# A fused transformer, attention and expert kernel: attention stacks transposed by DMA, key tiles taken in pairs, routing spread over two heads

## The reference, cut to what matters

```python
h = tok(x)                    # 8x8 patch convolution: 4 images x 256 tokens of 128; 2 layers; head to 192
h = concatenate([h, txt])     # 4 x 384 = 1536 rows of 192
h = h + attn(layernorm(h))
h = h + ffn(layernorm(h))

# attn; q and v are h @ W + b, reshaped to (NH = 12, BN = 1536, HD = 16)
q = q / maximum(norm(q), 1e-12)
AB = einsum('hnd,hmd->hnm', q, q)
AA = sum(q * q, axis=-1, keepdims=True)
sim = -(AA - 2.0 * AB + swapaxes(AA, -1, -2)) * HD ** (-0.5)
out = einsum('hnm,hmd->hnd', softmax(sim), v)

# ffn: t is the rmsnorm of its input; 16 experts, each row goes to its best 4
top_vals, top_idx = top_k(t @ gate_w.T + gate_b, 4)
route_w = softmax(top_vals)
out = sum over the 4 of route_w * (mlp2(swiglu(mlp1(t))))
```

## Time and profile before

| | us |
|---|---|
| median of 3 runs | 745.86 (744.64 to 749.47) |
| the profiled execution | 744.08 |
| its span in the profile | 742.3 |
| image part, until the first scores | 0 to 235 |
| twelve heads, until the last weighted product ends | 242.5 to 467.6 |
| end of routing and the plan of the tiles | 467.6 to 499.5 |
| experts | 499.5 to 742.3 |

### The profile page before, as it was taken

One profiled execution on the slowest core, in us unless ns is written; L12 is line 12 of the kernel. 1 busy time (PEld: TensorE's weight loads), 2 busy tenths in 40 slices (PEclk: granted clock), 3 DMA queues, 4 the chain that ended last, 5 costly groups with the idle time before them and its releaser, 6 DMA issues.

```text
span 742.3 us, 17563 instructions
## 1 busy us (share of the span) xinstructions
PE 646.7 (87%) x5070; PEld 430.3 (58%) x5071; DVE 450.2 (61%) x1478; ACT 380.0 (51%) x721; POOL 350.4 (47%) x401
## 2 busy tenths in 40 slices
PE   5888899888883999999999999549999999999970
PEld 5776786678651222222222222338999999999960
DVE  0345857675665267777777763446776676767660
ACT  0323337433312799999999999203443444444330
POOL 3111323132332045555555544422778777777781
PEclk9999999999997899999999999759999999999995
DMA  8999999300021992000000000048988998888844
GB/s 331 405 347 300 338 334 319 136 1 1 12 64 53 381 318 101 30 30 30 30 30 30 31 31 33 30 163 265 255 238 232 248 252 231 233 257 235 227 63 76
DMA packets 46064, 124.74 MB, mean 168 GB/s; under 512 B 5243, under 2 KB 31292, under 8 KB 44748
## 3 DMA queue, kind: packets, MB, share of 16 engines
q1 hardware_dynamic: 32780, 108.92, 44.5%
q0 software_dynamic: 11696, 14.19, 9.8%
q10 hardware_dynamic: 1552, 1.18, 0.5%
HBM read 105.53 MB, written 58.42 MB: 221 GB/s over the span
## 4 chain that ended last, share of the span: by engine, by line
PE 59%; DVE 11%; DMA 11%; POOL 7%; issue 5%; ACT 4%; SPq 1%; DVEq 0%; ACTq 0%; POOLq 0%
PE ps L843 14%; PE ps L830 10%; PE ps L982 7%; DMA out<-mid 5%; PE ps L1011 5%; PE ps L992 4%; PE ps L684 3%; DMA odd_sum<-mid 3%; ACT mid L1104 2%; POOL rstd L467 2%; POOL mid L590 2%; DVE stat L1192 2%; DVE mid L1200 2%; PE ps L760 1%; PE ps L657 1%
## 5 line engine op out<-in xcount | busy, mean ns | idle before, releaser
L1104 ACT ACTIVATE mid<-ps 128x1536 f32<-128x1536 f32 x144 | 200.2, 1458 | 29.4 <-PE ps L830 29.4
L843 PE MATMUL ps<-mid 128*32 128x384 f32 x1152 | 123.9, 502 | 1.3
L982 PE MATMUL ps<-mid,big 128*128 128x128 f32 x756 | 99.2, 282 | 0.3 <-ACT mid L1130 0.3
L1534 DVE TENSOR_SCALAR mid<-ps,big 128x128 f32<-128x128 f32 x189 | 54.6, 345 | 69.2 <-PE ps L992 51.9
L982 PEld LDWEIGHTS ps<-mid,big 128*128 128x128 f32 x756 | 91.9, 194 | 4.3 <-ACT mid L1130 0.5
L590 POOL TENSOR_TENSOR mid<-mid 128x384 f32<-128x384 f32 x63 | 68.5, 1087 | 54.1 <-DVE mid L1543 33.5
L830 PE MATMUL ps<-mid 52*128 52x512 f16 x432 | 87.4, 386 | 5.5 <-ACT mid L1104 4.9
L1137 ACT ACTIVATE mid<-mid 128x384 f32<-128x384 f32 x63 | 32.9, 522 | 85.4 <-DVE mid L1534 84.1
L1011 PE MATMUL ps<-big,mid 128*128 x378 | 69.2, 330 | 3.2 <-POOL mid L590 2.9
L541 POOL DMA_INDIRECT expert_in<-big,slot_u x48 | 47.9, 998 | 46.5 <-DVE slot_u L1425 35.5
L1011 PEld LDWEIGHTS ps<-big,mid 128*128 128x128 f32 x378 | 60.4, 190 | 6.3 <-issue 6.2
(11 more groups left out here) (224 smaller groups left out, 1089.8 us busy)
## 6 DMA issues: line engine op xcount, KB each, us to landing
big<-w_cat SPq DMA_DIRECT2D x63, 576.0 KB, 4.0
expert_in<-expert_in SPq DMA_DIRECT2D x16, 1774.5 KB, 48.7
big<-expert_in SPq DMA_DIRECT2D x63, 136.5 KB, 3.6
big<-patches SPq DMA_DIRECT2D x3, 2048.0 KB, 20.5
w_cat<-w_a SPq DMA_DIRECT2D x1, 6144.0 KB, 32.8
big<-w SPq DMA_DIRECT2D x1, 4608.0 KB, 14.6
w_cat<-w_b SPq DMA_DIRECT2D x2, 1536.0 KB, 31.0
big<-patches SPq DMA_DIRECT2D x4, 512.0 KB, 7.4
```

Of the source, the lines that this page charges most:

```text
L843: last = nc.tensor.matmul(oacc[32 * g:32 * g + 32, 0:QW], vhead[par][:, kb, :], probs[kb % 3][:, g * QW:(g + 1) * QW], start=(kb == 0), st ...
L982: last = nc.tensor.matmul(banks[half][:, c * P:(c + 1) * P], w1_t[q][:, half * FF + c * P:half * FF + (c + 1) * P], xtT[r][:, 0:P], start= ...
L1104: nc.scalar.activation(probs[kb % 3], SETS[kb % 2], ACT.Exp, scale=0.5).then_inc(probs_ready, 1)
L1534: last = nc.vector.tensor_scalar(glu[r][:, c * P:(c + 1) * P], bank(1 + r)[:, c * P:(c + 1) * P], b1_cols[:, bass.ds(ex * 6 + c, 1)], 7.0, ...
```

## The change: what it does

1. **Second convolution in front.** `schedule()` swaps two entries, so that the convolution of image 1 comes before the transposes of image 0. Its patches are loaded in four pieces, ahead of the other small loads, and its two row tiles are computed together, piece by piece.
2. **Stacks transposed by DMA.** The PE transposes, the DVE copies and the half precision identity are gone. DVE writes each key column block twice (`key_both`) and two extra query blocks (`qry_more`), and SP issues two DMA transposes per head: 12 blocks of 128x128 for the keys, 8 for the queries. They wait for the stack (`stack_ready`) and until the scores of the head that used the same buffer are done. PE waits for them (`stack_in`) before the first scores of the next head, and DVE before it overwrites the source.
3. **Key tiles in pairs.** Per pair PE does scores kb+2, one step of routing, scores kb+3, weighted kb, weighted kb+1. There are four `probs` buffers.
4. **Routing over two heads.** In head n the output, norms and row of tile n-1 are made, and tile n-2 is transposed, chosen, ranked and scattered. The row and the slots have two buffers. DVE and POOL are reordered to suit; at the end the scatter of tile 10 goes behind the norm powers of tile 11.
5. **Weights in pieces.** `w2` comes in two halves, the copy of `w1_a` in four, that of `w1_b` in two, one piece behind each head's transposes on SP.

```diff
-    return [(*lane[slot - start], b, tiles) for slot in range(len(LANE) + NB - 1)
-            for start, lane, b, tiles in lanes if 0 <= slot - start < len(lane)]
+    order = [(*lane[slot - start], b, tiles) for slot in range(len(LANE) + NB - 1)
+             for start, lane, b, tiles in lanes if 0 <= slot - start < len(lane)]
+    order[1:3] = [order[2], order[1]]
+    return order
...
+        probs4 = carve(QS)
...
-        stk = mid[:, 5 * QS + 2 * KEYB * 32:5 * QS + 2 * KEYB * 32 + NH * STKW].bitcast(f16)
-        key_tok = stk[:, 0:NH * STKW].rearrange("p (h c) -> p h c", h=NH)
-        qry_tok = stk[:, NH * STKW:2 * NH * STKW].rearrange("p (h c) -> p h c", h=NH)
-        stack_pair = [t.rearrange("p (j i) c -> p j (i c)", i=2) for t in (key_tok, qry_tok)]
+        key_flat, qry_flat = stk[:, 0:NH * P], stk[:, NH * P:(NH + 8) * P]
+        key_both = key_flat.rearrange("p (h i c) -> p h i c", h=NH, i=2)
+        key_tok = key_both[:, :, 0, :]
+        qry_tok = qry_flat[:, 0:6 * P].rearrange("p (h c) -> p h c", h=NH)
+        qry_more = qry_flat[:, 6 * P:8 * P].rearrange("p (j c) -> p j c", j=2)
+        qry_late = qry_flat[:, 0:2 * P].rearrange("p (j c) -> p j c", j=2)[:, :, STKW:STKW + STK]
...
+            sp.dma_start(rows_sb, rows[:, 0:5 * D].broadcast_to([P, 5 * D])).then_inc(rows_in, 16)
+            for k in range(0, KT, KT // 4):
+                ks = slice(k, k + KT // 4)
+                sp.dma_start(patch_sb[1][:, ks, :], patches[1][:, ks, :]).then_inc(patch1_in[k * 4 // KT], 16)
+            for dst, src, s in ((cols_sb[:], cols, cols_in), (qkvw_sb, qkv_w, qkvw_in),
...
+            def stacks(n, par):
+
+                sp.wait_ge(stack_ready, n + 1)
+                if n >= 2:
+                    sp.wait_ge(scores_ready, (n - 1) * KEYB)
+                sp.dma_start_transpose(out=keysT[par].rearrange("c (h n) -> c h n", n=P), in_=key_flat).then_inc(stack_in, 16)
+                sp.dma_start_transpose(out=qrysT[par][:, 0:8 * P].rearrange("c (j n) -> c j n", n=P),
+                                       in_=qry_flat).then_inc(stack_in, 16)
...
+                if stage == "S2":
+                    sp.wait_ge(acc_taken, weights_read)
+                    stacks(0, 0)
...
-            sp.wait_ge(vhead_ready, 1)
-            sp.dma_start(w2_sb, w2).then_inc(w_in, 16)
-            sp.dma_start(cat[:, :, 0:768], w1_a.rearrange("p (e c) -> p e c", e=E)).then_inc(w1_joined, 16)
-            for half in range(2):
-                sp.dma_start(cat[HROW * half:HROW * half + CB, :, 768:W1C],
-                             w1_b[0:CB, :].rearrange("p (e c) -> p e c", e=E)[:, :, half * FF:(half + 1) * FF]
-                             ).then_inc(w1_joined, 16)
-
-            sp.wait_ge(tr_taken, tr_base(NT - 2))
             sp.dma_start(b2_sb, b2).then_inc(b2_in, 16)
-
-            sp.wait_ge(w1_joined, 16 * 3)
+            cat, wide = [t.rearrange(f"{a} c -> p e c", **k) for t, a, k in
+                         ((w1_cat, "(e p)", dict(p=P)), (w1_a.rearrange("p (e c) -> e p c", e=E), "e p", {}))]
+            narrow = w1_b[0:CB, :].rearrange("p (e c) -> p e c", e=E)
+            pieces = [(w2_sb[:, k * (E // 2) * 3 * C:(k + 1) * (E // 2) * 3 * C],
+                       w2[:, k * (E // 2) * 3 * C:(k + 1) * (E // 2) * 3 * C], w_in) for k in range(2)]
+            pieces += [(cat[:, e:e + 4, 0:768], wide[:, e:e + 4, :], w1_joined) for e in range(0, E, 4)]
+            pieces += [(cat[HROW * half:HROW * half + CB, :, 768:W1C], narrow[:, :, half * FF:(half + 1) * FF], w1_joined)
+                       for half in range(2)]
+            sp.wait_ge(acc_taken, TOK_ACC)
+            for n in range(1, NT):
+                stacks(n, n % 2)
+                if 2 <= n < 2 + len(pieces):
+                    dst, src, s = pieces[n - 2]
+                    sp.dma_start(dst, src).then_inc(s, 16)
...
+            def pool_head(n, par, old=True, prep2=True):
+
+                pool.wait_ge(oacc_ready, n)
+                head_v(n + 1, 1 - par)
+                if old:
+                    weights(n - 2)
+                if prep2:
                     norm_root(n + 2)
-                if not first:
-                    scatter(r, 1 - par)
+                route(n - 1)
+                route2(n - 1)
+                base_add(n - 1)
+                if old:
+                    scatter(n - 2, par)
...
+            def pe_head(n, par, old=True, last=False):
+                base = head_base(n)
+                first = isinstance(n, int) and n == 0
+
+                def ahead(kb):
+                    if kb < KEYB:
+                        scores(par, kb, n * KEYB + (kb - 1))
                     elif not last:
-                        if kb + 2 == KEYB:
-                            pe.wait_ge(tr_taken, base + (2 if first else 3))
-                        scores(1 - par, kb + 2 - KEYB, n * KEYB + (kb + 1))
+                        scores(1 - par, kb - KEYB, n * KEYB + (kb - 1))
+
+                for kb in range(0, KEYB, 2):
+                    if kb + 2 == KEYB and not last:
+                        pe.wait_ge(stack_in, n * 32 + 64)
+                    ahead(kb + 2)
+                    if first:
+                        pass
+                    elif last:
+                        if kb == 0: t_transpose(n - 2, par, base)
+                        if kb == 2: logits(base + 2)
+                        if kb == 8: t_transpose(n - 1, 1 - par, base + 4)
+                        if kb == 10: logits(base + 5)
+                    elif not old:
+                        if kb == 6: out_transpose(n - 1, base)
+                    else:
+                        if kb == 0: t_transpose(n - 2, par, base)
+                        if kb == 2: logits(base + 1)
+                        if kb == 6: out_transpose(n - 1, base + 3)
+                    ahead(kb + 3)
                     weighted(n, par, kb)
-                    if first:
-                        if kb == 5:
-                            pe.wait_ge(b1_ready, 1)
-                            stacks(0, n + 1, base)
-                        if kb == 8: stacks(1, n + 1, base + 1)
-                    elif not last:
-                        if kb == 1: out_transpose(r, base)
-                        if kb == 2: stacks(0, n + 1, base + 1)
-                        if kb == 5: stacks(1, n + 1, base + 2)
-                        if kb == 7: t_transpose(r, 1 - par, base + 3)
-                        if kb == 8: logits(base + 4)
-                        if kb == 10: ranks(r, base + 5)
-                    else:
-                        if kb == 1: out_transpose(r, base)
-                        if kb == 7: t_transpose(r, 1 - par, base + 1)
-                        if kb == 8: logits(base + 2)
-                        if kb == 10: ranks(r, base + 3)
+                    weighted(n, par, kb + 1)
+                    if last:
+                        if kb == 0: out_transpose(n - 1, base + 1)
+                        if kb == 4: ranks(n - 2, base + 3)
+                    elif old and not first:
+                        if kb == 4: ranks(n - 2, base + 2)
...
-                    if not isinstance(n, int) or n * KEYB + kb >= 3:
-                        act.wait_ge(probs_used, n * KEYB + kb - 2)
-                    nc.scalar.activation(probs[kb % 3], SETS[kb % 2], ACT.Exp, scale=0.5).then_inc(probs_ready, 1)
-                    if kb == 0 and not (isinstance(n, int) and n == 0):
+                    if not isinstance(n, int) or n * KEYB + kb >= 4:
+                        act.wait_ge(probs_used, n * KEYB + kb - 3)
+                    nc.scalar.activation(probs[kb % 4], SETS[kb % 2], ACT.Exp, scale=0.5).then_inc(probs_ready, 1)
+                    if kb == 1 and not (isinstance(n, int) and n == 0):
...
+                if not isinstance(n, int) or n:
+                    dve.wait_ge(stack_in, n * 32)
...
+                nc.vector.tensor_copy(key_both[:, :, 1, 0:50], key_tok[:, :, 0:50])
+                step(nc.vector.tensor_copy(pairs(qry_tok[:, :, 50:52]), halves(key_tok[:, :, 48:50])))
+                nc.vector.tensor_copy(qry_more[:, :, 0:STK], qry_late).then_inc(stack_ready, 1)
...
+            def dve_head(n, par, half, old=True, prep2=True):
+
+                base = head_base(n)
+                if old:
+                    tT_copy(base)
+                    choose(n - 2, base + 1)
+                if prep2:
                     prep_squares(n + 2)
-                if not last and prep2:
+                if old:
+                    weigh(n - 2, par)
+                    place(n - 2, par, base + 2)
+                output(n - 1, base + (3 if old else 0))
+                norm_stats(n - 1, 1 - par)
+                norm_square(n - 1, 1 - par)
+                norm_rows(n - 1, 1 - par, half)
+                if prep2:
                     prep(n + 2)
```

264 lines of the change are left out of this document (110 added, 154 removed).

## The result

The kernel after took 739.43 us (median; 732.13 to 743.45) beside 747.02 us of the kernel before (744.54 to 752.23): a ratio of 0.9882, 95% interval 0.9855 to 0.9909. It is 1.2% faster, and 22 us above the forecast of 717. But that is the result of one comparison, and this turned out to be the heart of the case.

| comparison | before, us | after, us | ratio (95%) |
|---|---|---|---|
| first | 747.02 | 739.43 | 0.9882 (0.9855 to 0.9909) |
| second | 748.91 | 743.41 | 0.9936 (0.9898 to 0.9973) |
| third | 746.09 | 721.50 | 0.9643 (0.9598 to 0.9687) |

The account below looks back on a forecast made before the run. PE was taken as the bound, ACT close behind. From 744.1 us, 19 for the heads, 3.2 for the convolution, 3.0 before attention and 1.7 at the end gave 717; own range 710 to 723, with rivals 707 to 730.

Parts of the forecast that it names:

- parts 4, 5: Before the heads: second convolution in front, 3.2 us earlier; stack copies and PE stacks gone before attention, 3.0 us.
- parts 1 to 3: Heads: stacks by DMA, key tiles in pairs, routing over two heads; 1.9 us less for each of ten, 19 us.
- part 6: After the last head: tile 11's residual comes about 3 us earlier, its weights wait behind scatters; 1.7 us gained.
- part 2: Heads: with key tiles in pairs PE needs 16.4 us, ACT 16.7; walking the order gives 17.0 us per head.
- part 3: Heads: routing spread over two heads adds no work, but makes a ring of 16.6 us in heads of 17.0.
- a clock under 1.00 in the heads: Sign named beforehand: if the clock in the heads fell under this, the forecast was wrong; no size given.
- the rival ring: Heads: stack preparation takes 30% more, giving 17.7 us per head and 724 in all; chance 0.2 with the rival pair.
- the rival pair: Heads: two successive weighted steps save nothing, giving 17.6 us per head, 724 in all; chance 0.2 with the rival ring.
- rival C: Heads: the transposes by DMA are slow, making the kernel slower than before; 781 us at 20 us landing; chance 0.08.
- the estimate of 26 us: Heads: 20 blocks transposed by DMA one after another, at 1309 ns each, per head; about 845 us in all.
- the ring: Heads: output transpose, norms, row, stack preparation, logits, next output transpose; 16.6 us long, hidden by half a microsecond.
- rival A: Heads: the ring or the pair is longer than thought, 6 to 7 us in ten heads, 724; chance 0.2.

Follow-up runs that it names:

- before_third: The kernel before, unchanged, run again in the third comparison: 745.16 us (one run).
- after_third: The kernel after, unchanged, run again in the third comparison: 721.50 us.
- singles: The kernel after with all scatters, but the pairs undone (scores of one key tile, weighted products of one, in turns): 729.22 us, 0.9801 of before.
- one_at_the_seam: The kernel after with a tile's scatters moved: one at POOL's head end, one behind the next head's V copy, two behind the norm's root: 729.07 us, 0.9760 of before.
- the spread one: The kernel after with two of a tile's scatters at POOL's head end, one behind the next V copy, one behind the norm's root: 720.30, 721.80 and 729.58 us.

## Why the prediction was right or wrong

Wrong by 22 us in the first comparison, outside its range; in the third, without late signals, the time of 721.5 lies inside it, 4.5 us above the forecast. Which of the two a comparison would give was not in the forecast's reach, so the third is no proof of it. But there the terms can be judged one by one, before_third against after_third (all in us from the start of the span), with what the first pair of traces gives beside it:

| stretch | forecast | third pair | first pair |
|---|---|---|---|
| to the transposed bias rows (parts 4, 5) | -6.2 | 241.17 to 236.62: -4.6 | -4.6 |
| from there to the first copy of the sums | 0 | 19.11 to 21.39: +2.3 | 19.34 to 19.17: -0.2 |
| eleven periods (parts 1 to 3) | -19 | 206.1 to 187.7: -18.4 | 206.1 to 203.1: -3.0 |
| to the first product of the experts' first layer (part 6) | -1.7 | 32.2 to 30.0: -2.2 | 32.4 to 32.0: -0.4 |
| experts | 0 | 244.7 to 245.3: +0.6 | 242.3 to 245.1: +2.9 |
| span | -26.9 | -22.3 | -5.3 |

**The step that failed** is the one of part 2: "Walking the order through a head with these durations [...] I get 17.0 us per head", with ACT going on behind PE without a wait. The durations are right; what the walk leaves out is that PE's signals can be more than two microseconds late while POOL issues indirect transfers. I had put the scatters at nothing, since part 3 "adds no work" and POOL was busy for 10.3 of 19 us only. In the trace that I read they did cost nothing, in the same kernel's second trace 0.3 us per head. My reading is that there PE's own work was the bound and ACT had 1.8 us of air; the run that was to test it, singles, met no late signals, so it isn't shown. In the kernel after the rows show that the lateness stops ACT and ACT stops PE (1.03 and 0.94 us in the rows above), and nine heads of the first comparison are slower than the same heads of the third: by 0.8 to 1.6 us each, and by 2.4 to 2.9 the three in which the clock was halved for a stretch as well; 15.4 us in sum, the whole difference of the heads. The forecast named its own sign for this, a clock under 1.00 in the heads, but no cause for it. That the rival ring or the rival pair was given a chance of 0.2 doesn't cover it: both were priced at 724, and neither made the 22 us.

Right by its steps: the stacks by DMA (640 KB landed in 4.9 to 5.7 us in the heads; forecast 5), so rival C did not happen. Here the trace is near what the page "Advanced Engine Details and Errata" of the Trainium skill says on the X-bar transpose, that such transfers are as fast as plain ones (the plain 576 KB took 4.0). It does not bear out the estimate of 26 us, which multiplied the 1309 ns of the page "VectorE: DVE Perf Modes" of the Trainium skill, on the three transpose paths, for one block by 20. The pairs: 17.8 to between 17.0 and 17.3, which is 0.5 to 0.8 of the 1.9 us per head; I had named both parts together.

Nearly right: the ring. It was to be hidden by half a microsecond; without late signals it shows in three of the heads with 0.43 to 0.49 us, some 1.2 us in sum. So rival A happened in small, and one_at_the_seam shows that no more slack was left.

Sizes that were off: parts 4 and 5 gave 4.6 of 6.2 us (5.9 in the second pair of traces, where before has the longest image part, 243.38 us). The second convolution itself moved as forecast (it starts at 16.5, 18.1 and 17.2 in the three traces; forecast 17.2). In the third pair the first head gave another 2.3 us back, at a granted clock of 0.76 between 237.04 and 258.01 us, where it was 0.88 in the first; why it was lower there stays open. Of the weights in pieces, "I see no gain in them either" was true against the kernel before; against the changed one it is wrong, as they save 14 to 17 us there (measured without the scatters). The 2.9 us of the experts in the first pair lie within what either kernel varies by: the kernel before took 242.3, 245.2 and 244.7 for them in its three traces, the kernel after 245.1, 243.2 and 245.3.

**What stays open.** Why one trace has late signals and another of the same kernel has not, and whether that is settled for a comparison or for each execution; what in an indirect transfer holds PE's signals back; and whether it is the signal alone or the end of the products too, since the trace records only their starts. Of the kernels run, the spread one is the best where signals are late (0.9735 of before, against 0.9882 and 0.9936 for the kernel after in other comparisons), and as good as the kernel after where they are not (0.9656 against 0.9643 in the same comparison). The two were never run beside each other in a comparison with late signals.

## What to carry to other kernels

Work that lies hidden was free here only while the two engines that hand over to each other had air (idle time in the handover): when a change takes the air away, ask of every unchanged instruction beside the handover what it costs at its worst, not what it cost in one trace. A second trace of the kernel before, from another comparison, would have shown heads of 19.3 instead of 18.93 us, and with it the lateness that became 15 us in the changed kernel. Where POOL's indirect transfers lie beside a tight handover, try them in ones and twos rather than four in a row, but not ahead of a step on which a ring hangs.

## What the runs showed of the hardware

- While POOL issued indirect transfers (0.96 to 1.23 us each, mostly 0.3 apart), TensorE's signals came late in some traces: after the start of their last product 2.06 instead of 0.39 us and 2.89 instead of 0.53 at the seam, and up to 4.15 instead of 0.39 behind the V copy. Price in this tight loop, at full clock: 0.5 to 0.8 us per head for two, 0.8 to 1.7 for four. Four plain transfers of 96 KB on SP's queue: nothing.
- After the first comparison, the effect was there in three (in every trace with scatters in the heads; kernel before at 748.9 to 749.3 us, its heads 19.2 to 19.4 us where they were traced) and in none of three others (743.8 to 746.1 us, 18.93 where traced), once each on the same chip. In the first comparison (747.0) the kernel after had it, and the trace of before had not.
- In kernels where PE waited some 1 us per head, stretches at half clock came in some of the heads: 17.7 to 18.7 us long with the waits alone, they took 19.9 at a mean clock of 0.91 and 21.2 to 22.6 at 0.84 to 0.85.
- Two transposing transfers, 20 blocks of 128x128 in half precision, had landed 4.9 to 5.7 us after the first was issued, in the heads of the kernel after and of the one without scatters; queued behind some 14 MB of weights, the first took 11.5 us to issue and 14.8 to land.
